# Attention tokens of two groups loaded transposed and normalized a feature a partition, in a decoder block on one core

## The reference

```python
x = x + attn(layernorm(x))                 # 16 heads of 32, causal, ALiBi slopes, logits capped 30*tanh(s/30)
x = x + cross(layernorm(x), ctx_2048)      # one head of 512, 128 memory tokens a sequence, masked softmax
x = x + ffn(layernorm(x))                  # 512 -> 1536 -> 512, SiLU gate, weights rounded to fp8 e4m3, scales
layernorm(x) = (x - mean) / sqrt(var + 1e-5)
```

## Time and profile before

| what | value |
|---|---|
| time, median of 3 runs | 548.51 us (548.11 to 548.83) |
| profiled execution, its own time | 548.14 us |
| its span | 546.3 us |
| TensorE busy | 538.8 us, 99% of the span |
| VectorE / ScalarE / GpSimd busy | 371.0 / 273.4 / 288.8 us |
| granted TensorE clock | full over the whole span |
| transposes of line 298 | 160 instructions, 18.2 us busy |

### The profile page before, as it was taken

One profiled execution on the slowest core, in us unless ns is written; L12 is line 12 of the kernel. 1 busy time (PEld: TensorE's weight loads), 2 busy tenths in 40 slices (PEclk: granted clock), 3 DMA queues, 4 the chain that ended last, 5 costly groups with the idle time before them and its releaser, 6 DMA issues.

```text
span 546.3 us, 10113 instructions
## 1 busy us (share of the span) xinstructions
PE 538.8 (99%) x3930; PEld 423.9 (78%) x3930; DVE 371.0 (68%) x715; ACT 273.4 (50%) x494; POOL 288.8 (53%) x261
## 2 busy tenths in 40 slices
PE   8999999999999999999999999999999999999997
PEld 8878888888888888888888888766686667866675
DVE  7999877888565985659898976355943668344422
ACT  5858876878765785756753442034501343023310
POOL 5298898975783658787795346134300343013310
PEclk9999999999999999999999999999999999999999
DMA  8961231453217110229664612100071001600001
GB/s 279 345 240 45 80 96 60 128 182 119 78 40 231 40 59 2 78 76 314 217 225 131 236 43 82 52 1 0 1 154 40 0 1 30 145 19 0 1 20 59
DMA packets 56031, 53.89 MB, mean 99 GB/s; under 512 B 15152, under 2 KB 37680, under 8 KB 55984
## 3 DMA queue, kind: packets, MB, share of 16 engines
q1 hardware_dynamic: 55984, 53.25, 31.0%
HBM read 36.46 MB, written 13.63 MB: 92 GB/s over the span
## 4 chain that ended last, share of the span: by engine, by line
PE 82%; POOL 10%; DVE 5%; issue 2%; ACT 0%; DVEq 0%; POOLq 0%
PE bank L303 33%; PE bank L480 23%; PE bank L500 16%; POOL q_w L776 2%; POOL q_w L774 2%; POOL probs L767 2%; POOL x_res L790 2%; PE bank L414 2%; PE bank L399 2%; PE bank L298 2%; PE bank L424 1%; DVE q_m L1293 1%; PE bank L519 1%; PE bank L352 1%; PE bank L388 1%
## 5 line engine op out<-in xcount | busy, mean ns | idle before, releaser
L303 PE MATMUL bank<-reduced 128*128 128x512 f32 x936 | 223.0, 394 | 0.3 <-DVE ctxT L1237 0.3
L303 PEld LDWEIGHTS bank<-reduced 128*128 128x128 f32 x936 | 172.9, 188 | 37.8 <-issue 0.9
L878 POOL TENSOR_TENSOR f_parts<-fused,f_parts 128x512 fp32r<-128x512 f32 x48 | 62.9, 1310 | 153.7 <-ACT f_parts L1136 153.7
L1118 ACT ACTIVATE tanh_g<-bank,half_gate 128x512 f32<-128x512 f32 x48 | 33.0, 687 | 141.0 <-PE bank L480 133.9
L500 PE MATMUL bank<-reduced,f_parts 128*128 128x512 f32 x384 | 88.6, 391 | 0.0
L500 PEld LDWEIGHTS bank<-reduced,f_parts 128*128 128x128 f32 x384 | 72.0, 188 | 15.2
L480 PE MATMUL bank<-reduced 128*128 128x512 f32 x288 | 72.0, 402 | 0.0
L1482 DVE SCALAR_TENSOR_TENSOR silu<-tanh_g,bank 128x512 f32<-128x512 f32 x48 | 32.8, 684 | 55.6 <-ACT tanh_g L1118 55.6
L480 PEld LDWEIGHTS bank<-reduced 128*128 128x128 f32 x288 | 54.1, 188 | 12.8
L767 POOL TENSOR_SCALAR_AFFINE_SELECT probs<-probs 128x1024 f32<-128x1024 f32 x32 | 36.7, 1153 | 38.9 <-ACT probs L945 38.9
L774 POOL TENSOR_TENSOR q_w<-q_w,q_m 128x512 f32<-128x512 f32 x36 | 49.6, 1379 | 7.8 <-DVE q_m L1295 7.8
(11 more groups left out here) (127 smaller groups left out, 737.1 us busy)
## 6 DMA issues: line engine op xcount, KB each, us to landing
quantized<-q_w SPq DMA_DIRECT2D x36, 256.0 KB, 3.3
reduced<-quantized SPq DMA_DIRECT2D x12, 512.0 KB, 7.0
memT_sb<-in_memT SPq DMA_DIRECT2D x16, 256.0 KB, 4.8
mem_sb<-in_mem SPq DMA_DIRECT2D x16, 256.0 KB, 5.2
out<-y_sb SPq DMA_DIRECT2D x16, 256.0 KB, 2.0
q_w<-in_gate_w SPq DMA_DIRECT2D x12, 256.0 KB, 3.1
q_w<-in_up_w SPq DMA_DIRECT2D x12, 256.0 KB, 3.2
x_res<-in_x SPq DMA_DIRECT2D x3, 1024.0 KB, 9.0
```

The lines of the kernel that those rows point to most:

```text
L303: ins = pe.matmul(dst, stationary, moving, start=(n == 0), stop=(n == len(pairs) - 1))
L878: pool.tensor_tensor(f_lo[:, f, :], fused[:, f % 2, :], f_hi[:, f, :].bitcast(F32), ALU.subtract).then_inc(f_lo_ready, 1)
```

## The change

The tokens of g = 2 and g = 3 ("the third and fourth group") are no longer transposed on TensorE. A second input, `x_turned`, holds the same tokens with a feature a partition, laid out by the host. SyncE loads a group of it (1 MB) into `xn1`. Mean and rstd of a token, which are columns with a token a partition, have to be along the free axis on every partition: ScalarE stores them to memory element by element (`store_rows`, two DMAs of 512 elements) and loads them back spread over all partitions (`load_rows`, 128 x 1024) into the first two tiles of `xn2`. VectorE subtracts the mean and multiplies by rstd for each feature block k (`part_center`, `part_scale`, 8 instructions a group), ScalarE copies the high part (`part_high`), VectorE makes the low part (`part_low`), now from SBUF. `qk_proj` for hg = 0 of these groups waits for each k by itself. `norm_shift` and ScalarE's `norm_apply` remain for the FFN's first group alone. `norm_scale(0, n)` moves to the end of the group before on GpSimd, `low_part(g, 0)` ahead of `causal(g, 2)`, the flags of hg = 2 behind the cross steps for g = 1 and 2, and the tables are changed: in g = 1 the slabs at hg = 0 to 3 become 3, 3, 1, 2 (rounded and prepared), and in g = 2 as well.

```diff
-ROUNDED = ((4, 1, 1, 2), (4, 4, 0, 2), (3, 3, 0, 2), (2, 3, 0, 2))
-FLAGGED = ((2, 1, 1, 2), (3, 5, 0, 2), (3, 3, 0, 2), (2, 4, 0, 2))
-PREPARED = ((4, 2, 1, 2), (4, 4, 0, 2), (3, 3, 0, 2), (2, 3, 0, 2))
+ROUNDED = ((4, 1, 1, 2), (3, 3, 1, 2), (3, 3, 1, 2), (2, 3, 0, 2))
+FLAGGED = ((2, 1, 1, 2), (2, 4, 0, 2), (4, 3, 0, 2), (3, 4, 0, 2))
+PREPARED = ((4, 2, 1, 2), (3, 3, 1, 2), (3, 3, 1, 2), (2, 3, 0, 2))
+        spread_norm = xn2[:, 0:2, :]
@@ TensorE
-                for i in range(GT):
-                    turn_x(g + 1, i, (S_BANK, S_BANK + 1, Q_BANK, K_BANK)[i])
+                if g in (0, G - 1):
+                    for i in range(GT):
+                        turn_x(g + 1, i, (S_BANK, S_BANK + 1, Q_BANK, K_BANK)[i])
@@ qk_proj
+                for k in range(KT):
+                    if g >= 2 and hg == 0:
+                        pe.wait_ge(xT_lo_ready, (g - 2) * KT + k + 1)
...
+                    if name == "K" and hg == HG - 1 and 0 < g < G - 1 and k < KT - 1:
+                        ins.then_inc(xT_read, 1)
@@ SyncE, at hg == 3 ahead of the slabs, g < G - 2
+            def load_turned(n):
+                if n == 2:
+                    wait_filled(sp, ("N", 1, GT - 1))
+                else:
+                    sp.wait_ge(xT_lo_ready, KT * (n - 2))
+                sp.dma_start(xn1[:], x_turned[n]).then_inc(xt_loaded, 16)
@@ GpSimd
             def add_bo(g, i):
-                pool.wait_ge(xn_ready[0], (g + 1) * GT)
+                if g < 2:
+                    pool.wait_ge(xn_ready[0], (g + 1) * GT)
+                else:
+                    pool.wait_ge(var_ready[0], (g + 1) * GT)
@@ -828 hg = 0
-                    norm_scale(0, g + 1)
@@ hg = 2
-                causal(g, 2, (0,))
                 if g:
                     low_part(g, 0)
+                causal(g, 2, (0,))
@@ hg = 3, last but the flags
+                if g < G - 1:
+                    norm_scale(0, g + 2)
@@ ScalarE
+            def store_rows(g):
+                act.wait_ge(rstd_ready[0], g)
+                row = norm_rows[g].rearrange("w (i s) -> w s i", i=GT)
+                act.dma_start(row[0], mv[0][:, :, 0], allow_slow_non_contiguous=True).then_inc(rows_stored, 16)
+                act.dma_start(row[1], rstd[0][:], allow_slow_non_contiguous=True).then_inc(rows_stored, 16)
+            def load_rows(g):
+                if g >= 3:
+                    wait_filled(act, ("T2", g - 3, GT - 1))
+                act.wait_ge(rows_stored, 32 * (g - 1))
+                act.dma_start(spread_norm.rearrange("p w n -> p (w n)"),
+                              norm_rows[g].rearrange("w n -> (w n)").partition_broadcast(P)).then_inc(rows_loaded, 16)
+            def part_high(g, k):
+                act.wait_ge(xt_scaled, (g - 2) * KT + k + 1)
+                if k < KT - 1:
+                    act.wait_ge(xT_read, (g - 2) * (KT - 1) + k + 1)
+                else:
+                    wait_filled(act, ("K", g - 1, HG - 1))
+                act.activation(xT_hi[:, k], xn1[:, k], ACT.Copy).then_inc(xT_hi_ready, 1)
@@ ScalarE's order, g = 1
+                    if g:
+                        store_rows(g + 1)
                     q_out(g, 1)
                     k_out(g, 1)
+                    if g:
+                        load_rows(g + 1)
@@ g >= 2: store_rows(g + 1) behind q_out(g, 1), load_rows(g + 1) behind cross_first(g - 2, 4)
@@ hg = 2, 0 < g < G - 1
+                    for k in range(3):
+                        part_high(g + 1, k)
+                    k_out(g, 3)
+                    context_high(g, 1)
+                    part_high(g + 1, 3)
@@ VectorE
+            def part_center(g, k):
+                if k == 0:
+                    dve.wait_ge(xt_loaded, 16 * (g - 1))
+                    dve.wait_ge(rows_loaded, 16 * (g - 1))
+                dve.tensor_tensor(xn1[:, k], xn1[:, k], spread_norm[:, 0], ALU.subtract).then_inc(xt_centered, 1)
+            def part_scale(g, k):
+                dve.wait_ge(xt_centered, (g - 2) * KT + k + 1)
+                dve.tensor_tensor(xn1[:, k], xn1[:, k], spread_norm[:, 1], ALU.mult).then_inc(xt_scaled, 1)
+            def part_low(g, k):
+                dve.wait_ge(xT_hi_ready, g * GT + k + 1)
+                dve.tensor_tensor(xT_lo[:, k], xn1[:, k], xT_hi[:, k].bitcast(F32), ALU.subtract).then_inc(xT_lo_ready, 1)
                 normalize_context(g, 0)
+                if 0 < g < G - 1:
+                    for k in range(KT):
+                        part_center(g + 1, k)
+                        part_scale(g + 1, k)
@@ hg = 1
-                    norm_shift(g + 1)
+                    if g == G - 1:
+                        norm_shift(G)
@@ hg = 2
                 for i in range(GT):
-                    x_low(g + 1, i)
+                    if 0 < g < G - 1:
+                        part_low(g + 1, i)
+                    else:
+                        x_low(g + 1, i)
```

57 lines of the change are left out of this document (39 added, 18 removed).

## The result

The changed kernel takes 562.62 us (median of 6 runs, 560.68 to 563.79) against 548.40 before: a ratio of 1.0251, 95% interval 1.0238 to 1.0264. The forecast was 552.6, at most 556.0. The profiled execution took 563.79 us, the longest of the six; its span is 562.0.

A forecast was written before the change was run, and what follows sets the result against it. TensorE, 99% busy, was taken as the bound, with new waits for VectorE outweighing the removed transposes: 2.9 (g=1) + 1.3 (g=2) + 0.3 (ScalarE) = 4.5 us on 548.14, so 552.6 us; range 546.0 to 556.0.

The forecast's parts named there:

- What ScalarE gets and loses: ScalarE, g=1: row stores land in 3.3 us, last v_out done at 83.9, needed near 84.4; cost nothing.
- Its own sign of being wrong: Forecast wrong if TensorE stays gapless, the eight VectorE instructions take under 7 us, or the largest wait names ScalarE or DMA.
- rival 3: Row stores land late (over 4 us), holding v_out(1,3) and context(1,0): +3 us on the forecast, 555 to 559; chance 10%.
- Costs from there one for one: ScalarE, g=1: row stores landing slower than assumed delay context(1,0) by the same amount, beyond half a us of cover.
- What leaves TensorE: Sixteen transposes leave TensorE in g=1 and in g=2, with the gap behind them at g=1: 3.0 us together if nothing is late.
- near tie: The chain of waits through GpSimd for much of the second group's stretch, taken as no gap on TensorE.
- rival 1: VectorE's additions fit at their free pace, the eight taking 5.3 us: 545.1 to 547 us; chance 20%.
- The first stall, context(1,1): g=1: VectorE's eight instructions beside GpSimd empty the bank at 105.2 to 105.7, TensorE wants it at 102.60; stall 2.6 us.
- The second stall, context(1,3): g=1: VectorE needs 21.4 us, with part_low and norm_apply stretched beside GpSimd, against TensorE's 19.5; stall 1.9 to 2.0 us.
- g=2: Same stalls with GpSimd less full: 1.0 us, then 1.6 us, less 1.33 us of transposes; sum +1.3 us.
- The change of groups: g=2: row store issues on ScalarE ahead of cross(0,2) delay the low part TensorE reads; 0.3 us (0 to 1.0).
- SyncE's queue: load_turned(3), behind slab 20, lands at 152 and is read at 155.3: costs nothing, cover 3 us.

The follow-up runs named there:

- the normalization for nothing: Changed kernel with norm_apply split and no row stores, row loads, centring or scaling, third and fourth group's tokens left unnormalized: 548.19 us, ratio 0.9992 to the kernel before.
- the later load: Changed kernel with only ScalarE's load_rows in g=1 moved from ahead of context_high and the four v_out to behind them: 555.47 us, ratio 1.0130 to the kernel before.

## Why the prediction was wrong

**What ScalarE gets and loses: the step that failed.** The forecast put this term at "nothing, by half a us": the row stores were taken to land in 3.3 us, by a row of 256 KB stores, with v_out(1,3) just in time. They took 9.2 and 10.8; at g=1 they were issued at 74.05 and 74.46, and ScalarE went on at 84.37, where the forecast had 78.0. The last two v_out started at 88.80, where it had them done at 83.9. Its own sign of being wrong, a largest wait that names ScalarE or a DMA, is what the traces have. The mechanism stood in the text as rival 3, with a bound of 11 us; but the value was taken from the nearest row, which is a store of another shape (256 KB, not 2 KB in 512 single elements), and rival 3 got 10% and 3 us, up to 559. Measured price: 7.15 us (562.62 - 555.47), since ScalarE's delay also set GpSimd's rounding and VectorE's centring 5.9 us later (97.18 against 91.32). "Costs from there one for one" held at context(1,0), 4.88 us; further on it grew.

**What leaves TensorE: right as a count, wrong as a gain.** 1.62 and 1.2 us did leave the intervals. But "nearly every instruction taken from it counts one for one" fails: with the normalization for nothing the time fell by 0.46 us (the interval of the ratio ends at 1.0000), and by 0.9 with the slabs moved as well. A TensorE busy for 99% was not the only bound: once 1.6 us were out of it, GpSimd's masks (0.83), VectorE's ctxT (1.02) or x_pT_lo (1.5) were waited for, by where the slab stood. The chain of waits through GpSimd, which the forecast called a near tie, was that tie. In the sum for the changed kernel the error is small, since there VectorE sets the starts. It is rival 1, 545.1 to 547, that none of these schedules reached, even with nothing to pay for the normalization.

**The first stall, context(1,1): right.** Forecast 105.2 with 2.6 us of stall; with the landing out of the way 105.17 and 2.25. The eight instructions took 9.2 us (91.32 to 100.53), forecast 91.15 to 100.7. That this fits so closely is in part luck: five ran beside GpSimd, in 0.81 and 1.46 to 1.80 us, where the forecast had four at 1.75.

**The second stall, context(1,3): right in its cause, a little small.** Forecast 1.9 to 2.0; 2.04 in the changed kernel, 2.06 with the later load, from part_low 4.68 (forecast 4.7) and norm_apply 5.62 (4.8). Taking work from ahead of it removed it. The wait of 0.51 us for tile xn ahead of it was not forecast, and from context(1,2) to (1,3) the way was 2.75 us longer than before.

**g=2: half right.** The stall at context(2,1), 1.0 us, did not occur (170.00 - 150.24 = 19.76 us from context(2,0) before, 183.40 - 163.64 = 19.76 in the changed kernel): the addition that empties the bank ended at 183.28, just in time, as VectorE's idle time ahead of it was used up. The stall at context(2,3), 1.6: 2.02 in the changed kernel, 1.36 with the later load.

**The change of groups: a second term sized too small.** 0.3 us was taken for x_pT_lo. With the later load the way from context(1,3) to (2,0) was 2.26 us longer than before, 0.43 of it the wait for x_pT_lo; most of the rest lies where the granted clock was 0.58, behind the 2.06 us wait (128 to 132 us). The way from (2,3) to (3,0) was 0.8 us longer as well. These two, with the 0.5 for xn and less the 1.0 of g=2, are most of the 2.9 between 555.5 and 552.6. Another execution of that kernel, with a mean clock of 1.000 where the traced one has 0.995, took as long (555.32 and 555.35 us). That speaks against the slow stretch as the cause; what the cause is stays open.

**SyncE's queue: right.** Nothing waited for x_turned (7.6 us to land).

## What to carry to other kernels

A store's landing time is to be read from a store of the same shape: if none is in the trace, the far bound is the value to plan with, and nothing that others need goes behind the wait for it. An engine at 99% is a bound only together with those that arrive just in time; before its work is cut, take the work out and replace it with nothing (a run that leaves it out): here that gives 0 to 0.9 us of 3.0, less than any of the replacements tried here cost. A wait removed shows only at the next point where the engines meet, so read gains at several milestones to the end, not at the first.

## What the runs showed of the hardware

Two KB to memory in 512 runs of 4 bytes landed in 7.3 to 10.8 us (medians of two issues each, in four kernels), in 128 runs of 16 bytes in 2.8 and 3.3; 16 KB in 128 runs of 128 bytes in 4.1 to 5.1. A VectorE instruction of 128 x 512 fp32 with both operands in SBUF takes 0.69 us alone and mostly 1.46 to 1.80 beside GpSimd (the first of the eight 0.81 and 0.84); with one of them read at a step of 16 bytes 1.07 and up to 2.17. GpSimd's two add_bo took 3.43 to 3.47 us in such company, where two take 2.91 in the earlier trace rows. VectorE's 32 x 32 turn of 128 x 32 fp32 took 0.20 us.
